# Placing the keys into strips from ScalarE's DMA queue, the queries from the shared one

## What is computed

```
x = layer_norm(h);  q, k, v = x @ w_qkv.T            # 16 heads of 16
q, k = rope(layer_norm per head of q and k)
h2 = h + softmax(q k^T / 4) v @ w_proj.T + b_proj
y = layer_norm(h2)
out = h2 + y @ W_lin.T + b_lin + sum over the 2 best of 8 experts of weight_e * (y @ left_e @ right_e)
```

## Time and profile before

| what | value |
|---|---|
| median of 3 runs | 846.07 us (845.97 to 848.58) |
| the profiled execution's own time | 839.57 us |
| span of its instructions | 837.5 us |
| mean granted clock of TensorE | 0.932 |
| PE busy | 714.7 us, 85% of the span |
| ACT busy | 406.3 us, 49% |
| DVE busy | 551.5 us, 66% |
| POOL busy | 426.5 us, 51% |
| hardware DMA queue | 24.6% of what 16 DMA engines could give |

### The profile page before, as it was taken

One profiled execution on the slowest core, in us unless ns is written; L12 is line 12 of the kernel. 1 busy time (PEld: TensorE's weight loads), 2 busy tenths in 40 slices (PEclk: granted clock), 3 DMA queues, 4 the chain that ended last, 5 costly groups with the idle time before them and its releaser, 6 DMA issues.

```text
span 837.5 us, 23778 instructions
## 1 busy us (share of the span) xinstructions
PE 714.7 (85%) x9335; PEld 571.8 (68%) x9335; DVE 551.5 (66%) x1225; ACT 406.3 (49%) x974; POOL 426.5 (51%) x449
## 2 busy tenths in 40 slices
PE   3978768898985526799999999999999999999984
PEld 3867656787863314678777777777787777777752
DVE  3554536687768233668778688787778878878542
ACT  2443223353431123566656566666666676566531
POOL 3544714556452066644744654755754665565311
PEclk9988889999997566999999999999999999999997
DMA  9920582141000031212122123122122222211200
GB/s 203 229 68 1 181 233 54 30 84 36 7 1 6 7 97 34 59 47 68 31 57 66 46 64 73 44 67 69 41 74 60 56 61 58 54 33 32 53 24 27
DMA packets 69476, 53.02 MB, mean 63 GB/s; under 512 B 36127, under 2 KB 68598, under 8 KB 69238
## 3 DMA queue, kind: packets, MB, share of 16 engines
q1 hardware_dynamic: 69366, 51.50, 24.6%
HBM read 33.69 MB, written 11.40 MB: 54 GB/s over the span
## 4 chain that ended last, share of the span: by engine, by line
PE 32%; DMA 11%; SPq 10%; DVE 5%; issue 3%; ACT 2%; POOL 1%; DVEq 0%; POOLq 0%; ACTq 0%
DMA out<-out_sb 9%; PE p_c L1311 7%; PE p_a L1311 7%; PE p_s L1368 3%; SPq L1066 3%; SPq L1067 3%; PE p_o L1377 3%; PE p_n L1385 2%; SPq L1056 2%; PE p_s L1352 2%; PE p_c L1422 2%; PE p_a L1335 2%; SPq L1050 2%; PE p_c L1403 1%; PE p_s L1364 1%
## 5 line engine op out<-in xcount | busy, mean ns | idle before, releaser
L1103 POOL TENSOR_TENSOR t<-t,ss_rs 116x512 f32<-116x512 f32 x48 | 51.0, 1062 | 143.8 <-ACT ss_rs L1150 143.6
L1243 DVE TENSOR_REDUCE mx<-p_s 87x16 bf16<-87x1392 f32 x64 | 102.3, 1598 | 13.2 <-PE p_s L1352 12.6
L421 POOL TENSOR_TENSOR xs_lo<-xcols,xs_hi 120x585 fp32r<-120x585 f32 (+1 forms) x45 | 63.8, 1428 | 71.8 <-ACT xs_hi L473 71.8
L1173 ACT ACTIVATE prT<-p_s 87x1392 f32<-87x1392 f32 x64 | 85.0, 1328 | 31.5 <-PE p_s L1368 31.5
L1099 POOL TENSOR_TENSOR t<-t 116x512 f32<-116x512 f32 x48 | 61.0, 1271 | 41.8 <-DVE t L1234 41.7
L1368 PE MATMUL p_s<-qr,kr 32*87 32x87 f32 x2048 | 68.8, 257 | 0.0
L1106 POOL TENSOR_TENSOR t<-t,tabs 116x512 f32<-116x512 f32 x48 | 61.1, 1274 | 1.5
L1368 PEld LDWEIGHTS p_s<-qr,kr 32*87 32x87 f32 x2048 | 60.3, 154 | 0.0
L1311 PE MATMUL p_c<-w_f,yT 128*116 128x296 f32 x192 | 56.8, 419 | 1.7 <-ACT f L1198 0.6
L1364 PE MATMUL p_s<-mxT,pick_row 32*87 32x87 bf16 x1024 | 55.7, 208 | 1.1 <-ACT mxT L1169 1.1
L1311 PE MATMUL p_c<-w_p,onT 128*116 128x256 f32 x192 | 55.1, 411 | 1.2 <-ACT yT L1192 0.9
(11 more groups left out here) (250 smaller groups left out, 1968.5 us busy)
## 6 DMA issues: line engine op xcount, KB each, us to landing
xcols<-in_x_cols SPq DMA_DIRECT2D x12, 822.7 KB, 10.5
h<-h_tokens SPq DMA_DIRECT2D x16, 348.0 KB
out<-out_sb SPq DMA_DIRECT2D x48, 116.0 KB
h_tokens<-in_txt SPq DMA_DIRECT2D x1, 4928.0 KB, 20.7
x<-in_txt_cols SPq DMA_DIRECT2D x32, 154.0 KB, 3.3
qr<-qkT SPq DMA_DIRECT2D x64, 58.0 KB, 2.0
kr<-qkT SPq DMA_DIRECT2D x64, 58.0 KB, 2.0
xcols<-in_x_cols SPq DMA_DIRECT2D x3, 759.4 KB, 6.0
```

The lines of the kernel that those rows point to most:

```text
L421: nc.gpsimd.tensor_tensor(xs.lo[:, n % XS_SLOTS, :, 0:M].bitcast(F32R), raw, xs.hi[:, n % XS_SLOTS, :, 0:M], ALU.subtract).then_inc(S['xs_ ...
L1103: link(nc.gpsimd.tensor_tensor(t4, t4, ss_rs[:, b].unsqueeze(2).broadcast_to([TP, 2 * HEADS, HD]), ALU.mult))
L1173: nc.scalar.activation(prT[:, k % 2], p_s[0:SEQ, :, 0:QUADS * SEQ], ACT.Exp, scale=HD ** -0.5).then_inc(S['s_exp'], 1)
L1243: nc.vector.reduce_max(mx[:, k % 2, :, 0:QUADS], p_s[0:SEQ, :, 0:QUADS * SP].rearrange("p j (a k) -> p j a k", k=SP)[:, :, :, 0:SEQ], AX_X ...
```

## The change

The four `kr` DMAs of each part leave SP's program. ACT's order gets two new entries, `place.1.2` and `place.0.1`, each right behind the `qkT` copy whose columns complete the part, and ACT issues the four DMAs there, after waits on its own copy and on the scores of the group before last. SP keeps the `qr` DMAs, its order and its waits. Both count the same `k_in` semaphore, and nobody else's waits change.

```
 ORDER_ACT = order("""... exp.3.3 qkT.2.2 place.1.2 rstd_r.0.1 ffn.2.4
...
-                    yT.1.3 oT.1.2 exp.2.2 qkT.1.1 rstd_c.0.3""")
+                    yT.1.3 oT.1.2 exp.2.2 qkT.1.1 place.0.1 rstd_c.0.3""")
...
                     for a in range(QUADS):
                         r = slice(64 * (a % 2), 64 * (a % 2) + 64)
                         sp.dma_start(qr[0:P:2, half, a, c0:c1], qkT[r, half, a // 2, c0:c1]).then_inc(k_in[half][k], 16)
-                        sp.dma_start(kr[0:P:2, half, a, c0:c1], qkT[r, half, 2 + a // 2, c0:c1]).then_inc(k_in[half][k], 16)
...
+                if name == 'place':
+                    if g < 2:
+                        act.wait_ge(S['set_0'], QR_KR_SET)
+                    wait(act, S['qkT_out'], 3 * g + k + 2)
+                    wait(act, S['s_mm'], GB * (g - 1))
+                    c0, c1 = K_COLS[k]
+                    for a in range(QUADS):
+                        r = slice(64 * (a % 2), 64 * (a % 2) + 64)
+                        nc.scalar.dma_start(kr[0:P:2, half, a, c0:c1], qkT[r, half, 2 + a // 2, c0:c1]).then_inc(k_in[half][k], 16)
```

More of the change, by code:

```diff
@@ L939 @@
                     oN.0.2 mT.2.2 pv.1.2 yT.1.3 scores.2.2 proj.2.3 qkT.1.1 oN.1.2 ffn.0.3 peak.3.2""")
-ORDER_ACT = order("""ffn.0.4 rstd_r.2.2 oB.0.3 sq.0.1 ffn.1.4 mT.3.3 oT.2.3 oB.1.3 yT.2.4 exp.3.3 qkT.2.2 rstd_r.0.1 ffn.2.4
+ORDER_ACT = order("""ffn.0.4 rstd_r.2.2 oB.0.3 sq.0.1 ffn.1.4 mT.3.3 oT.2.3 oB.1.3 yT.2.4 exp.3.3 qkT.2.2 place.1.2 rstd_r.0.1 ffn.2.4
                     sq.1.1 mT.0.2 oB.2.3 rstd_a.0.1 oT.3.3 exp.0.2 v.0.2 v.1.2 gate.0.4 mT.1.2 v.2.2
                     yT.0.3 v.3.2 exp.1.2 qkT.0.1 rstd_r.1.1 twT.0.4 oT.0.2 oB.3.3 sq.2.1 mT.2.2 xhi.0.0
-                    yT.1.3 oT.1.2 exp.2.2 qkT.1.1 rstd_c.0.3""")
+                    yT.1.3 oT.1.2 exp.2.2 qkT.1.1 place.0.1 rstd_c.0.3""")
 ORDER_DVE = order("""stats.0.0 ss.2.2 max.3.3 eps.0.1 rotate.0.1 norm.2.3 ss.0.1 stats.1.0 max.0.2 rotate.1.1 logits.0.4
```

## The result

| what | before | after |
|---|---|---|
| median, measured together | 847.33 us | 881.12 us (873.47 to 890.18) |
| ratio | | 1.036, 95% interval 1.028 to 1.044 |
| span of the profiled execution | 837.5 us | 871.4 us |
| mean granted clock | 0.932 | 0.928 |
| PE busy in 500 to 600 us | 97.4 us | 92.8 us |

The kernel became slower by about 31 us. The direction was forecast, the size was not: I had said +16. A later measurement beside other kernels gave 1.050 (1.044 to 1.057); the two intervals only touch, so the change costs 3 to 5%. Some executions of a kernel fall into a second, slower state; all ratios here go by the faster ones, and so can differ a little from the quotient of the medians beside them.

What follows compares the result with a forecast made beforehand. The prediction took PE's order, 93 to 97% busy, as the bound. Stalls of 13 x 1.87 = 24.3 us less a gain of 8.1 made +16.2 us, from 846.07 to 862 us, with a range of 840 to 890.

Steps and rivals of the forecast that it cites:

- What bounds it: From 340 us on PE's order is the bound, busy 93 to 97%; anything making PE wait is paid nearly in full.
- What it gives (8.1 us): SP's shorter queue removes PE's waits: 6.0 us behind `out_sb` and its store, 2.1 us for keys.
- The price of an issue: Four key DMAs hold ACT 2.43 us from the copy's end, taken from the same DMAs issued by SP.
- Part 0 (0.73 us): PE's `ffn.1.4` waits for ACT's late `f`: 0.73 us an iteration, a hold of 2.43 less 1.70 of slack.
- rival 2: SP's and ACT's queues take turns: fully, hold 4.98 us and 929 us; partly, hold 3.2 and 882 us; chance 0.15.
- Part 1 (1.14 us): `proj.0.3` waits for `f`, `lora` for `h2`; the hold leaves PE 1.14 us later an iteration.
- POOL's cover: Behind part 0, POOL's late `scale` and `shift` still end before the `qkT.2.2` transposes need them, with 0.7 us of cover.
- How often (13): The stalls of 1.87 us count in 13 of 14 iterations, 24.3 us; the last, in the tail, costs nothing.
- The sum: Stalls of +24.3 us less a gain of 8.1 make +16.2 us: 862 us on the median, 1.9% slower.
- SP's relief: Rival, chance 0.20: with ACT issues under 0.45 us the gain exceeds the stalls; 838 us at holds of 1.29 or less.
- the slack of 1.70: In part 0, how late ACT's `f` can be before PE's `ffn.1.4` is held: 1.70 us.
- the formula: PE's stall per iteration for an ACT hold W: (W - 1.70) in part 0 plus (W - 1.29) in part 1.

Runs made afterwards that it cites:

- the bursts apart: The change, with SP's queries of part 0 waiting until ACT's burst is over; 876.40 us, ratio to the kernel before 1.046 (1.040 to 1.051).
- the second trace of the change: The change itself measured again, nothing altered, beside the kernel before: 882.82 against 844.74 us, ratio 1.050 (1.044 to 1.057).
- the kernel without keys: The kernel before with the key DMAs left out, so scores are not computed: 836.42 against 838.73 us, ratio 0.996 (0.993 to 1.000).

## Why the prediction was right and wrong

*What bounds it: right.* PE was full, ACT's queue was the one that could hurt it, and of PE's 36.5 us of waits in the change from 340 to 800 us 29.9 are waits for `f`.

*What it gives (8.1 us): right in its places, its size open.* The waits for `out_sb` and for keys went away. In most iterations the ruler shows 0.3 us. Measured alone, the relief is worth 3 us (0 to 6).

*The price of an issue: right for a lone queue.* I took 2.43 us for four; ACT's bursts take 2.41 us where SP's doesn't start with them ("the bursts apart"), and 2.42 in part 1, where SP's loses the common start. SP's rows were a good stand-in for ACT's.

*Part 0 (0.73 us): too low, it measured 1.24.* The step that failed reads "I take this hold of 2.43 us". In part 0 both queues wake at the same semaphore, and ACT's burst takes 2.75. That is 0.34 us of the missing 0.51; part 0 with the collision moved away adds 0.90. I had the collision as rival 2, in full (4.98 us, 929 us) or in part in every issue (3.2 us in both parts, 882 us), and left it out of the forecast. That the median of 881 us lies at the milder one's time is chance: its holds aren't there, ACT's bursts take 2.75 and 2.42 us. The one shared start had no price of its own. Of the other 0.17, the copy `f` started 0.62 us after `c_ln` and not 0.56, and the matmuls after the gap took 1.25 us in place of 1.16.

*Part 1 (1.14 us): right, it measured 1.23.* Even the detail held that `lora` keeps a smaller wait for `h2`: 0.20 us instead of 0.42. POOL's cover held too: its `scale` starts 1.05 us behind the start of `f`, where I had 1.06. (My words "as before" there were wrong: before the change `scale` followed `f` by 1.69 us.)

*How often (13): the step that failed with it.* "The last falls into the tail, where PE no longer is full", so I counted it as nothing. It cost 6.9 us by the ruler. In a full iteration three pairs of `qk` matmuls of a later group stand between the `peak` and `ffn.1.4` (604.74 to 606.37 us), and three more before `proj.0.3`; in the tail no such group is left, and the two gaps are 2.38 and 2.29 us, 4.7 together. The rest is the slower matmuls behind them. In the second trace of the change it cost 5.3. Sparse work there was taken for cover; it was the opposite.

*The sum.* On the profiled executions: 13 x 2.47 = 32.1 for the stalls in place of 24.3, +6.9 for the last group in place of 0, and 2.2 us after the last `peak`. Against this stand 8.9 us in the same 13 iterations (9.8 gained at the store, less 0.9 by which the two places cost more than 13 x 2.47) and 1.0 us before the eighth `peak`; I had 8.1. The remaining 2.5 us lie ahead of the first `peak` and are not the change's.

The 9.8 us need care. 6.5 of them come from two iterations of the trace before, in which the step with the wait for `out_sb` took 11.74 and 11.83 us; in the change, and in the kernel without keys, it takes 8.5. PE there, before the change, in the first of the two:

```profile
432.46 0.43 PE L1403 MATMUL p_c<-ident,h 116*128 116x116 f32 x2 [1.61 <-DVE out_sb L1294]
...
434.74 1.80 PE L1311 MATMUL p_c<-w_p,onT 128*116 128x256 f32 x4
```

A gap of 1.6 us is followed by matmuls of 1.80 us in place of 1.12, at a granted clock of 0.50 (434 to 436 us). The change removes this gap, so the longer matmuls behind it may be part of the gain; whether every execution of the kernel before has them its one trace doesn't tell, and the relief measured alone over ten executions was 3 us and not 10. The gain may thus be a third term that I took too high.

The forecast was short by about half, mostly through two terms that I had named and sized wrongly: the shared start (with what goes along with it in part 0, 13 x 0.51 = 6.6 us) and the tail (6.9 us).

*The rivals.* SP's relief does win, but only with bursts of two: with two issues the hold of 1.3 to 1.4 us is under the slack of 1.70 in part 0 and at the 1.29 in part 1, as the formula says. With the four of the change, relief never had a chance at 0.6 us an issue.

## What to carry to other kernels

A queue's issues can be moved to a compute engine only as far as the slack of the instructions behind them goes: read how long the next result can be late before the bound engine waits, divide by the issue's row, and move that many. Here it was two of four, and three and four cost 0.6 us each. When two queues wait for the same semaphore, count one lost start; when a queue is made later to avoid it, look at what it meets next. And price the thin end of a pipeline by itself: here the same burst stalled PE twice as long there.

## What was not expected of the hardware

Two queues that start a burst together do not alternate: one of them loses 0.3 us once (2.75 against 2.41 us for four issues), and which one it is stays the same from iteration to iteration for a given place. Once in each trace of the change the burst of part 1 took longer on both queues (ACT's 3.5 us at 418 us, and 3.2 us at 489 us); why is open. Small SBUF-to-SBUF DMAs that mostly land in 2.0 us took up to 6.5 when issued beside larger loads and stores.

The granted clock stayed at 1.00 with gaps of 1.0 to 1.2 us twice an iteration. Longer gaps had no fixed sequel: behind those long bursts PE's gap was 2.27 us in the first trace, and the clock stayed at 1.00; it was 2.00 us in the second, and the clock was 0.50 from 495 to 499 us. Behind the gaps of 1.6 us before the change it fell as well. With gaps of 3.4 to 4.3 us twice an iteration it was 0.86 to 0.91 on average.
